# Mean and variance of the first LayerNorm: from VectorE statistics to running sums on ScalarE

## What is computed

```
h = layernorm(x) * (1 + ca) + sa            # mean and variance over the 256 features
y_f = sigmoid(mamba(h));  y_b = sigmoid(mamba(reversed h))     # 512 channels, 16 states
x1 = x + ga * (layernorm(0.5 * (y_f + y_b)) * ln_g + ln_b + h)
out = x1 + gb * ffn(layernorm(x1) * (1 + cb) + sb)
```

## Time and profile before

| | |
|---|---|
| median of 3 runs | 4685.21 us (4684.75 to 4686.28) |
| the profiled execution, its own time | 4683.44 us |
| its span, first to last instruction | 4681.6 us |
| busy share, PE / PEld / DVE / ACT / POOL | 95% / 72% / 81% / 70% / 71% |
| a chunk of the first pass (2 to 13), scan to scan | 103.30 to 103.33 us |
| a chunk of the second pass (19 to 30), scan to scan | 101.66 to 101.93 us |
| feed-forward stage | from about 3370 us to the end |

### The profile page before, as it was taken

One profiled execution on the slowest core, in us unless ns is written; L12 is line 12 of the kernel. 1 busy time (PEld: TensorE's weight loads), 2 busy tenths in 40 slices (PEclk: granted clock), 3 DMA queues, 4 the chain that ended last, 5 costly groups with the idle time before them and its releaser, 6 DMA issues. The chain is left out here.

```text
span 4681.6 us, 69073 instructions
## 1 busy us (share of the span) xinstructions
PE 4451.6 (95%) x24932; PEld 3375.9 (72%) x24932; DVE 3800.5 (81%) x4136; ACT 3279.4 (70%) x7067; POOL 3321.1 (71%) x1599
## 2 busy tenths in 40 slices
PE   8999999999999999999999999998899999999999
PEld 3676666667666666776666676666688888888888
DVE  6999999999999999999999999999754545444442
ACT  6788888888888877888888888888544444444443
POOL 5999999999999999999999999999710000000000
PEclk9999999999999999999999999999999999999999
DMA  8545444444554444444444445445411101010100
GB/s 296 175 136 150 146 142 138 141 136 140 148 146 138 147 138 140 136 143 143 138 139 132 135 137 147 142 134 158 164 62 35 34 23 37 32 37 32 37 23 10
DMA packets 297752, 545.90 MB, mean 117 GB/s; under 512 B 101888, under 2 KB 186624, under 8 KB 262784
## 3 DMA queue, kind: packets, MB, share of 16 engines
q1 hardware_dynamic: 296512, 529.91, 37.3%
q10 hardware_dynamic: 896, 11.54, 0.7%
HBM read 502.77 MB, written 50.14 MB: 118 GB/s over the span
## 5 line engine op out<-in xcount | busy, mean ns | idle before, releaser
L1472 DVE TENSOR_TENSOR_SCAN m_h<-bank,m_dBx 128x512 f32<-128x512 f32 x1728 | 2004.3, 1203 | 112.3 <-ACT bank L1205 82.4
L904 PEld LDWEIGHTS bank<-ident,m_h 128*128 128x128 f32 x8192 | 972.1, 142 | 514.5 <-issue 370.5
L904 PE MATMUL bank<-ident,m_h 128*128 128x128 f32 x8192 | 1203.6, 276 | 63.8 <-DVE m_h L1480 50.4
L1363 POOL TENSOR_TENSOR m_dBx<-u,m_Bs 128x1024 f32<-128x1024 f32 x432 | 1019.2, 2385 | 1.1 <-DVE m_h L1472 0.9
L1363 POOL TENSOR_TENSOR m_dBx<-m_u,m_Bs 128x1024 f32<-128x1024 f32 x432 | 1018.5, 2384 | 0.0
L1374 POOL TENSOR_TENSOR m_h<-m_h,m_Cs 128x1024 f32<-128x1024 f32 x384 | 912.7, 2377 | 37.9 <-ACT m_state L1119 37.4
L1480 DVE TENSOR_TENSOR m_h<-m_h,bank 128x1024 f32<-128x1024 f32 x640 | 768.9, 1201 | 22.8 <-PE bank L886 16.9
L311 POOL TENSOR_TENSOR mvj<-mvj,norm_c 128x4 f32<-128x4 f32 x16 | 16.6, 1035 | 970.9 <-DVE mvj L272 970.9
L1205 ACT ACTIVATE bank<-dt,cols 128x511 f32<-128x511 f32 (+1 forms) x864 | 593.5, 689 | 19.0 <-DVE m_h L1472 18.3
L1205 ACT ACTIVATE bank<-m_dt,cols 128x511 f32<-128x511 f32 (+1 forms) x864 | 593.6, 689 | 18.7 <-DVE m_h L1472 18.1
L886 PEld LDWEIGHTS bank<-ident,m_Ct 128*128 128x128 f32 x2560 | 303.5, 138 | 336.1 <-issue 212.7
(11 more groups left out here) (189 smaller groups left out, 5933.7 us busy)
## 6 DMA issues: line engine op xcount, KB each, us to landing
m_Bs<-b_dram SPq DMA_DIRECT2D x256, 1024.0 KB, 5.4
m_Cs<-c_dram SPq DMA_DIRECT2D x384, 256.0 KB, 3.5
m_dg<-d_dram SPq DMA_DIRECT2D x160, 256.0 KB, 3.7
xx<-in_x SPq DMA_DIRECT2D x16, 512.0 KB, 5.4
xn_dram<-xx SPq DMA_DIRECT2D x16, 512.0 KB, 3.3
yb_dram<-m_ysb SPq DMA_DIRECT2D x16, 512.0 KB, 3.3
xx<-xn_dram SPq DMA_DIRECT2D x16, 512.0 KB, 3.8
x_dram<-m_ysb SPq DMA_DIRECT2D x16, 512.0 KB, 3.3
```

What stands on the lines that cost most here:

```text
L904: mm = pe.matmul(YB[b][:, o:o + P], h[:, k % NH, m, tok:tok + P], ident[:, :], start=(s == 0 and o == 0), stop=False, is_transpose=True, s ...
L1363: pool.tensor_tensor(dBx[:, dbx_ring(ch, k) % NDBX, :, :], u[ch.batch][:, m, :], Bs[:, k // BP % 2, k % BP, :].unsqueeze(1).broadcast_to(( ...
L1472: dve.tensor_tensor_scan(o, decays, share, initial, ALU.mult, ALU.add).then_inc(S["scan"], 1)
```

## The change

In the bodies of chunks 0 to 13 DVE's eight statistics instructions go. ACT takes them over in two places. At step 6 (AT_SUM) `sum_x` passes the four 128x256 tiles of x through a copy in place that also writes each row's sum. At step 12 (AT_SQ) `square_x` scales the sums to the negated mean (one small instruction, and a wait for it), and then passes the four tiles through Square with that mean as bias, which writes each row's sum of centred squares; the squares themselves go to xn as scratch. POOL's `norm_sums` does three small steps rather than four. `norm_x` reads its factor from another column. The prologue keeps the old way.

```diff
+AT_SUM, AT_SQ = 6, 12
+            def sum_x(ch):
+                act.wait_ge(S["x_in"], ch.at(16, 16))
+                for t in range(TS):
+                    ins = act.activation(xy[:, t, :], xy[:, t, :], ACT.Copy, accum_out=mv[:, t, 0:1])
+                ins.then_inc(S["ln"], 1)
+            def square_x(ch):
+                wait(act, S["xn_out"], ch.at(16, 0))
+                act.sem_inc(S["go"], 1)
+                wait_filled(act, ch.go(-1), J_LN[1])
+                act.sem_inc(S["go"], 1)
+                act.wait_ge(S["ln"], ch.at(LNK, 1))
+                act.activation(mv[:, :, 1], mv[:, :, 0], ACT.Copy, scale=-1.0 / DM).then_inc(S["ln"], 1)
+                act.wait_ge(S["ln"], ch.at(LNK, 2))
+                for t in range(TS):
+                    ins = act.activation(xn[:, t, :], xy[:, t, :], ACT.Square, bias=mv[:, t, 1:2], accum_out=mv[:, t, 2:3])
+                ins.then_inc(S["ln"], 1)
...
-                for s in range(TS):
-                    ins = act.activation(xn[:, s, :], xy[:, s, :], ACT.Identity, scale=mv[:, s, 3:4], bias=mv[:, s, 5:6])
+                r = 3 if ch.number() < 2 else 4
+                for t in range(TS):
+                    ins = act.activation(xn[:, t, :], xy[:, t, :], ACT.Identity, scale=mv[:, t, r:r + 1], bias=mv[:, t, 5:6])
...
+                    if k == AT_SUM and norms(ch, 2):
+                        sum_x(ch.go(2))
+                    if k == AT_SQ and norms(ch, 2):
+                        square_x(ch.go(2))
...
+            def norm_sums(ch):
+                pool.wait_ge(S["ln"], ch.at(LNK, 3))
+                pool.tensor_scalar(mv[:, :, 3], mv[:, :, 2], 1.0 / DM, EPS, ALU.mult, ALU.add).then_inc(S["ln"], 1)
+                pool.wait_ge(S["ln"], ch.at(LNK, 4))
+                pool.tensor_tensor(mv[:, :, 4], mv[:, :, 3], norm_c[:, 1, :], ALU.pow).then_inc(S["ln"], 1)
+                pool.wait_ge(S["ln"], ch.at(LNK, 5))
+                pool.tensor_tensor(mv[:, :, 5], mv[:, :, 1], mv[:, :, 4], ALU.mult).then_inc(S["ln"], 1)
...
-                        norm(ch.go(2))
+                        norm_sums(ch.go(2))
...
-                    if norms(ch, 2):
-                        norm(ch.go(2), k)
```

## The result

| | before | after |
|---|---|---|
| median of 14 runs each | 4684.45 us (4683.30 to 4686.72) | 4694.22 us (4692.86 to 4696.36) |
| profiled execution, its own time / its span | 4683.44 / 4681.6 us | 4696.36 / 4694.5 us |
| a chunk of the first pass (2 to 13), scan to scan | 103.30 to 103.33 us | 104.10 to 104.13 us |
| chunk 14 | 103.33 us | 104.90 us |
| a chunk of the second pass (19 to 30) | 101.66 to 101.93 us | 101.66 to 101.71 us |

The change makes the kernel slower by 9.8 us, a ratio of 1.0021 with a 95% interval of 1.0013 to 1.0029. The interval lies above 1, so the sign is clear; the size sits on the 0.2% that were called the edge of what can be told. The forecast was 4703.8 us, 19.4 above before, so the effect is half of what was forecast.

A forecast was written before the change was run, and what follows sets the result against it. A ring of waits through PE, ACT and DVE was taken as the bound, not DVE or POOL. Squares delaying PE 1.43 us in 13 chunks add 18.6 to 4683.44; with 1.77 to the median, 4703.8 us, range 4686 to 4728.

The forecast's parts named there:

- the ring: Chain of waits among PE, ACT and DVE that closes after one chunk; norm_x its only norm work, worth up to 1.97 us.
- s: Price of one ACT copy with running sum over a 128x256 tile in sum_x: 0.47 us (0.28 to 0.67).
- q: Price of one ACT Square with running sum over a 128x256 tile in square_x: 0.58 us (0.39 to 0.78).
- 4q - 0.89: PE's delay a chunk if held from the second transpose before convolution 0: 1.43 us, the reading taken.
- 4q - 1.22: PE's delay a chunk if held only from convolution 0, the reading not taken.
- the likeliest case: The forecast that the kernel gets 9.4 to 35 us slower, 4694 to 4721 us; chance 0.62.
- Chunk 0: First chunk, said to pay nothing: 2.86 us of ACT idle time ahead of step 13 holds square_x's 2.5 us.
- Cheap sums: Rival: running sums add nothing on ACT, PE held at convolution or transposes, 4690 to 4694 us; chance 0.15.
- DVE is the bound: Rival: DVE's scans pace the stretch, so its 1.6 us come off 13 chunks, 4664 us; chance 0.09.
- knock-ons: Rival mechanisms beyond the squares' delay, a PE clock drop or ACT table loads; 0.14 together with dearer sums, over 35 us.
- a table load for Square: Rival: ACT loads a table before and after the squares, 2 x 1.28 us a chunk, 33 us in all, 4737 us.
- The clock's fall: Rival: PE drops from 2.4 to 1.2 GHz behind its new wait, losing some 1.8 us more a chunk, 23 us, 4727 us.

The follow-up runs named there:

- e1: The changed kernel with the sums at ACT's step 5 and the squares at step 8, where ACT idled: 4685.36 us, ratio 1.0002.
- e2: The changed kernel with the squares one step later, at step 13, behind the copy of input product 2: 4684.42 us, ratio 1.000.
- e5: The changed kernel with the four squares done twice in the same place, a wait between the two: 4731.53 us, one run.
- e4: The kernel before with DVE's eight statistics instructions left out of chunks 0 to 13, nothing given to ACT, mean and variance stale: 4684.42 us, ratio 1.0001.
- e3: The changed kernel with only the sums moved, from step 6 to step 5, squares left at step 12: 4695.29 us.
- e8: The changed kernel with the squares but without their running sum, so the variance is stale: 4690.69 us.
- e6: The changed kernel with sums at step 5, squares at 8, POOL's steps after unit 6 and norm_x at step 15: 4677.57 us, ratio 0.9985.
- e7: The kernel before, DVE's statistics kept, with POOL's norm after unit 7 and norm_x at step 16: 4678.58 us, ratio 0.9987.
- e11: e10 with POOL's power left out, so the factor is stale: 4663.65 us.
- e12: e10 with POOL's first small step, scaling and epsilon, done by ACT behind the squares: 4671.62 us, ratio 0.9971.
- e9: e6 with two of POOL's three small steps on DVE, only the power left on POOL: 4692.58 us, ratio 1.002.
- e10: e6 with POOL's three steps after unit 7 instead of 6 and norm_x at step 16 instead of 15: 4676.44 us, ratio 0.9985.

## Why the prediction was right, and where its sizes were off

**Right: direction, place and mechanism.** PE's wait for DVE's product, ACT's evacuation, convolution 0, `norm_x`, the decays and the scan form the ring; the squares enter it at the copy of input product 2 (L1047). Moving them to either side of that place brings the loss to zero (e1, e2), and doubling them adds 2.1 us for 2.0 us of work and a wait of 0.1 (e5).

**Right at zero.** DVE's 1.6 us (e4: ratio 1.0001, the scan at 420.41 unmoved), the sums at step 6 (e3: 104.1 us as after), POOL's shorter norm, and the load of x, for which no wait appeared in the bodies. ACT's idle time before L1058 stayed near 1 us, as forecast. Two signs came out smaller than forecast: DVE's idle time grew by 1.8 us a chunk and not by 3, since its busy time fell by 1.0 and not by 1.6, and POOL's grew by 0.9 and not by 1.7. Neither lies on the ring; why DVE's busy time fell by so little was not taken apart.

**The sums' price.** s was taken as 0.47 and measured 0.40, q as 0.58 and measured 0.495. The passes were priced nearly right and the read wrong: it is 0.19 us long, as assumed, but overlaps both neighbours and adds only 0.10. The Trainium skill's rule that was cited (VectorE: DVE Perf Modes, Two Vector instructions with no wait between them: an accumulator output makes two instructions) holds for ScalarE too by these rows; it gives no time for the read or its overlap, and the overlap was half the cost assumed for it.

**Where PE is held: the mis-sized term.** The text offered 4q - 0.89 (hold at the transposes) and 4q - 1.22 (hold at the convolution) and took the first. With q = 0.495 they give 1.09 and 0.76; measured were 0.74 at PE and 0.80 in the chunk. The transposes at 402.01 were not held. The reading of the program was right, that of the recorded wait wrong. The text took 0.16 us from the end of the copy to the next matmul, with no row for it; here it is 0.14 (403.04 to 403.18). Together, 13 x 1.43 = 18.6 us became 12 x 0.80 + 0.72 (chunk 1) = 10.3. Of the missing 8.3 us, 13 x 4 x (0.58 - 0.495) = 4.4 are the price and 13 x 0.33 = 4.3 the place, less 0.5 for the 0.04 us between 0.76 and 0.80. Both misses went the same way, so they did not cancel: the measured effect is half the forecast, at the lower edge of the likeliest case's own range (4694 to 4721).

**Chunk 0.** It was expected to pay nothing. In this pair of profiles chunk 1 begins 1.0 us later. But its start lies between 172.2 and 177.7 us in the profiles of all kernels, the first scan between 71.6 and 76.2, and in e3, with the squares in the same place, chunk 1 begins at 172.45, ahead of before's 173.64. So the traces do not say whether chunk 0 pays.

**The rivals.** *Cheap sums* (4690 to 4694) had its premise wrong, since the read is not free (e8: 0.4 us for four), but was right that PE is held only at the convolution; the measured 4694.2 lies at its upper edge as much as at the forecast's lower one. *DVE is the bound* is excluded by e4. Of the *knock-ons*, a table load for Square did not occur: the profile has the same 64 loads under the decays' line (1.28 us each) and none under L1174 or L1161. This bears on the rule of the Trainium skill that was cited (ScalarE: Activation LUTs, Table sets): Square behaves here like those it names. The clock's fall behind the new wait occurred in no chunk of after, at a wait of 0.74 us, but in four of twelve in e5, at 2.86 us, for 1.69 us each where the text put 1.8.

**The rule on cheap elementwise work** (the Trainium skill, ScalarE: Activation LUTs, Rules for kernel authors) spoke against the change. The runs bear it out less than the sign suggests: at steps 5 and 8 or 6 and 13 ACT's 3.6 us of passes cost nothing against DVE's 1.6. Here the place decided, not the engine.

**Wrong, later on: what bounds the ring once `norm_x` is off it.** The expectation for e6 put the chunk at 101.7 to 101.9 us, by the second pass, and that for e7 at 101.9 to 102.2. They were 102.7 and 102.8: POOL, with its 1.4 us of small steps in e6 and one wait of 0.57 us left, became the bound, as e11 shows by taking one of them out and e12 by moving another. The expectation for e9 counted DVE's two small steps at nothing, and they took 3.7 us a chunk. What holds e12 at 102.26 rather than 101.7 was not taken apart further; POOL's power and last product (1.05 and 0.21 us) are still there. In e11, too, POOL's idle time is 0.8 us as in e10, so which engine bounds it was not shown.

## What to carry to other kernels

Work moved to an engine with idle time costs what it does to the instruction behind it that another engine waits for, less that instruction's slack, so it is put just behind that instruction or ahead of an idle stretch. Relief of a busy engine is worth nothing where that engine only waits longer afterwards for another one. When a piece leaves the ring, ask which engine is next and how much idle time it has in one round; here that was POOL, 0.6 us behind.

## What the runs showed of the hardware that had not been expected

- ACT's read of a running sum (128x1) is 0.19 us long and adds 0.10 to the pitch. Square on 128x256 with one pointer operand lasts 0.50 us with or without the sum; the copy with it 0.41. A plain copy of that size (PSUM to SBUF) lasts 0.37.
- A DVE tensor_scalar on 128x4 elements of SBUF, 0.17 us with POOL idle, lasts 2.30 us on average (0.98 to 2.94) beside POOL's products of 2.3 us (e9): it ends 0.02 to 0.03 us after one of them. bn_stats on 128x256 takes 0.41 us beside POOL or without it.
- PE's spells at 1.2 GHz come in about every other chunk of the first pass, behind an early wait, and cost nothing there. One came behind a later wait in chunk 14 of after (2.10 us between the last transpose's slot and the next matmul, 1.94 in the row), and one behind the new wait of 2.86 us in chunks 2, 4, 8 and 12 of e5. Each time it fell on the ring it cost 1.6 to 1.7 us. What makes it land where it does stays open.
